# A pass for the maximum of a hidden layer: work of VectorE and ScalarE divided anew over three engines

## The reference, cut to what matters

```python
def bitnet_linear(x, W, b):
    w_scale = jnp.maximum(jnp.mean(jnp.abs(W)), 1e-05)
    qW = jnp.sign(W) * (jnp.abs(W) > 0.5 * w_scale).astype(W.dtype)
    i_scale = jnp.maximum(jnp.max(jnp.abs(x)), 1e-08) / 127.0
    qx = jnp.clip(jnp.round(x / i_scale), -128.0, 127.0)
    out = jnp.einsum('...i,oi->...o', qx, qW) * (w_scale * i_scale)
    return out + b
...
avg_img = jnp.mean(image_embeds, axis=1, keepdims=True)
concatenated = jnp.concatenate([fused, jnp.broadcast_to(avg_img, (b, s, e))], axis=-1)
h = jax.nn.relu(bitnet_linear(concatenated, W_f1, b_f1))     # 512 -> 1024
return bitnet_linear(h, W_f2, b_f2)                          # needs max |h| first
```

## Time and profile before

| | us |
|---|---|
| median of 3 runs | 1606.0 (1601.48 to 1606.73) |
| span of the profiled execution | 1604.8 |
| PE busy in it | 1374.0 (86%) |
| DVE busy | 1164.6 (73%) |
| ACT busy | 942.2 (59%) |
| POOL busy | 341.6 (21%) |
| the pass, from its first memset to its last reduction | 1194.94 to 1274.41 |

### The profile page before, as it was taken

The page is one execution under the profiler, slowest core; times in us unless marked ns, Lnnn a source line. Parts: engine busy times, 40 slices in busy tenths (PEclk is TensorE's granted clock), DMA queues, the critical chain, the costliest instruction groups (busy, mean ns, idle before and its releaser), DMA issues. The chain is left out here.

```text
span 1604.8 us, 25713 instructions
## 1 busy us (share of the span) xinstructions
PE 1374.0 (86%) x8272; PEld 1087.8 (68%) x8315; DVE 1164.6 (73%) x3017; ACT 942.2 (59%) x1434; POOL 341.6 (21%) x311
## 2 busy tenths in 40 slices
PE   8566779999999999999999777548868779999996
PEld 2345667888888888888888666435632247777775
DVE  6535666767887777778787844429969868898895
ACT  3333354566566675676656445369947057877873
POOL 2012111111221212121221100077200042433320
PEclk9767789999999999999999999869979889999998
DMA  7661033434554555445556675343200011111211
GB/s 218 144 234 39 25 118 124 141 129 151 180 165 146 173 163 164 151 148 165 173 174 223 204 227 169 131 128 108 60 2 0 5 48 40 61 60 54 67 53 40
DMA packets 114561, 192.64 MB, mean 120 GB/s; under 512 B 18256, under 2 KB 83360, under 8 KB 114400
## 3 DMA queue, kind: packets, MB, share of 16 engines
q1 hardware_dynamic: 96352, 146.18, 29.4%
q0 software_dynamic: 13824, 43.81, 7.9%
q10 hardware_dynamic: 4256, 1.07, 0.3%
HBM read 134.10 MB, written 57.98 MB: 120 GB/s over the span
## 5 line engine op out<-in xcount | busy, mean ns | idle before, releaser
L1268 ACT ACTIVATE hr_r<-pair 128x512 f32<-128x512 f32 x136 | 80.1, 592 | 141.4 <-PE pair L167 139.7
L165 PE MATMUL pair<-kv_ring,hr_lo 128*128 128x256 f32 x544 | 158.5, 291 | 4.1 <-DVE hr_lo L3216 4.1
L166 PE MATMUL pair<-kv_ring,hr_hi 128*128 128x256 f32 x544 | 154.3, 284 | 0.0
L167 PE MATMUL pair<-kv_ring,hr_hi 128*128 128x256 f32 x544 | 154.2, 284 | 0.0
L165 PE MATMUL pair<-th_hi,kv_ring 128*128 128x512 f32 x272 | 115.4, 424 | 42.1 <-issue 39.0
L4443 ACT ACTIVATE ff<-pair,hbs,s1h 128x512 f32<-128x512 f32 x128 | 96.4, 774 | 77.8 <-PE pair L4753 72.9
L4397 POOL DMA_INDIRECT ff<-x_scratch,slots x64 | 78.2, 1222 | 224.2 <-POOLq L3895 141.1
L1070 POOL DMA_INDIRECT rows_scratch<-row,slot x64 | 68.7, 1074 | 221.3 <-DVE slot L3155 163.5
L3216 DVE TENSOR_TENSOR hr_lo<-hr_sq,hr_hi 128x512 fp32r<-128x512 f32 x136 | 93.3, 688 | 26.9 <-ACT hr_sq L1282 12.6
L165 PEld LDWEIGHTS pair<-kv_ring,hr_lo 128*128 128x128 f32 x544 | 104.3, 192 | 10.6 <-DVE hr_lo L3216 5.4
L166 PE MATMUL pair<-th_lo,kv_ring 128*128 128x512 f32 x272 | 109.3, 402 | 0.0
(11 more groups left out here) (420 smaller groups left out, 4212.6 us busy)
## 6 DMA issues: line engine op xcount, KB each, us to landing
kv_ring<-expert_scratch SPq DMA_DIRECT2D x136, 512.0 KB, 3.9
acc_s<-rows_scratch SPq DMA_DIRECT2D x17, 528.0 KB, 5.3
xn_s<-rows_scratch SPq DMA_DIRECT2D x17, 512.0 KB, 5.0
x_scratch<-acc_s SPq DMA_DIRECT2D x17, 512.0 KB, 4.4
text_scratch<-text SPq DMA_DIRECT2D x17, 512.0 KB, 5.3
x_in<-in_x SPq DMA_DIRECT2D x16, 512.0 KB, 4.8
expert_scratch<-expert_space POOLq DMA_DIRECT2D x2, 4096.0 KB, 18.4
out<-ff SPq DMA_DIRECT2D x16, 512.0 KB, 2.9
```

The costliest lines, as they stand in the source:

```text
L165: pe.matmul(dst, st[1], mv[0], start=start, stop=False, skip_group_check=True)
L166: pe.matmul(dst, st[0], mv[1], start=False, stop=False, skip_group_check=True)
L167: return pe.matmul(dst, st[0], mv[0], start=False, stop=stop, skip_group_check=True)
L1268: s.activation(hr_r[:, c % 2, :], up_ps[:, (c % 2) * T:(c % 2 + 1) * T], ACT.Relu).then_inc(relu_done, 1)
```

## The change

The 16 samples, the matmuls and what is computed stay. The work after the matmuls and the rounding are divided otherwise:

- Pairs 0 and 1 (four chunks, `NR` = 4) are reduced by VectorE from PSUM as before.
- Pairs 2 and 3 are copied by **ScalarE** to SBUF as 16-bit integers (`whole`, two buffers; all values are whole numbers and fit). VectorE then halves them three times with an elementwise maximum (1024 elements a partition, 512, 256), each step waiting for the one before, and reduces the 256 that are left. This `fold` of sample n-1 stands behind the two reductions of sample n.
- The second rounding step, which subtracts the constant, goes to **GpSimd**. `qy` gets a second buffer. ScalarE's first step runs two samples ahead and stands in its list between the copies of two samples: rounded(n+2), then the copies of sample n.
- The copies of sample n wait until the fold of sample n-2 has freed their buffer. TensorE waits for pairs 2 and 3 on ScalarE's copies, for 0 and 1 on VectorE.
- All loops are written out.

```diff
-        qy = sb("qy", [P, KC * T])
+        qy = [sb(f"qy{h}", [P, KC * T]) for h in range(2)]
...
+                @block.gpsimd
+                def _(g):
+                    def quantised(n):
+                        g.wait_ge(hy_done, n + 1)
+                        g.tensor_scalar(qf[:, n, :, :].rearrange("p k t -> p (k t)"), qy[n % 2][:, :], ROUND, None, ALU.subtract).then_inc(hq_done, 1)
+                    for n in range(B):
+                        quantised(n)
...
-                        s.wait_ge(hy_done, n + 1)
-                        s.activation(qf[:, bass.ds(n, 1), :, :].rearrange("p o k t -> p (o k t)"), qy[:, :],
-                                     ACT.Identity, bias=neg_round[:, :]).then_inc(hq_done, 1)
...
+                    def evict(n):
+                        after(s, folded_, n - 1)
+                        for q in range(NR // 2, HC // 2):
+                            s.wait_ge(h_done, HC // 2 * n + q + 1)
+                            at = 2 * q - NR
+                            s.activation(whole_[n % 2][:, at:at + 2, :].rearrange("p c t -> p (c t)"), psum[q][:, :], ACT.Copy).then_inc(evicted, 1)
...
+                        if n + 2 < B:
+                            rounded(n + 2)
+                        evict(n)
...
+                    def fold(n):
+                        v.wait_ge(evicted, NE // 2 * (n + 1))
+                        w, st = whole_[n % 2], Steps(v, fold_steps, 3 * n)
+                        st.add(v.tensor_tensor(half_[:, :, :], w[:, :, 0:T // 2], w[:, :, T // 2:T], ALU.max))
+                        st.wait()
+                        st.link(v.tensor_tensor(quarter[:, :, :], half_[:, :, 0:T // 4], half_[:, :, T // 4:T // 2], ALU.max))
+                        st.link(v.tensor_tensor(eighth[:, :, :], quarter[:, :, 0:T // 8], quarter[:, :, T // 8:T // 4], ALU.max))
+                        v.tensor_reduce(hall[:, NR:HC, n:n + 1].rearrange("p c o -> p (c o)"), eighth[:, :, :], X, ALU.max).then_inc(folded_, 1)
```

More of the change, by code:

```diff
@@ L18 @@
 F32, F32R, BF16, I32 = mybir.dt.float32, mybir.dt.float32r, mybir.dt.bfloat16, mybir.dt.int32
+I16 = mybir.dt.int16
 ALU = mybir.AluOpType
@@ L4233, in build @@
             hy_done, hq_done, h_done, h_red = sem("hid_rounded"), sem("hid_quant"), sem("hid_f1"), sem("hid_reduced")
+            evicted, folded_, fold_steps = sem("hid_evicted"), sem("hid_folded"), sem("hid_fold_steps")
             neg_round, pos_round = sb("neg_round", [P, 1]), sb("pos_round", [P, 1])
+            NR = 4
+            NE = HC - NR
             hall = sb("hall", [P, HC, B])
+            whole_ = [sb(f"whole{h}", [P, NE, T], I16) for h in range(2)]
+            half_ = sb("half", [P, NE, T // 2], I16)
+            quarter = sb("quarter", [P, NE, T // 4], I16)
+            eighth = sb("eighth", [P, NE, T // 8], I16)
             qya = sb("qya", [P, KC, B])
@@ L4247, in _ @@
                     pe.wait_ge(acc_ready, 1)
[L4249 removed]
+                    for n in range(B):
+                        pe.wait_ge(hq_done, n + 1)
                         for q in range(HC // 2):
[L4251 to L4253 removed]
+                            if q < NR // 2:
+                                after(pe, h_red, NR // 2 * (n - 1) + q + 1)
+                            else:
+                                after(pe, evicted, NE // 2 * (n - 1) + q - NR // 2 + 1)
                             for c in (2 * q, 2 * q + 1):
@@ new lines, in _ @@
+                    s.wait_ge(round_set, 2)
+                    rounded(0)
+                    rounded(1)
+                    for n in range(B):
+                        if n == 2:
+                            s.wait_ge(l_loaded, 48)
+                            for k, name in enumerate(("rT", "kT", "vT")):
+                                s.activation(lw[name][0][:, :, :], lstg[:, k, :, :], ACT.Copy, scale=0.5 if name == "vT" else 1.0).then_inc(lhi_done, 1)
+                        if n + 2 < B:
+                            rounded(n + 2)
+                        evict(n)
@@ L4294, in _ @@
[L4294 to L4301, removed]
@@ new lines, in _ @@
+                    for n in range(B):
+                        if n == 2:
+                            for k, name in enumerate(("rT", "kT", "vT")):
+                                v.wait_ge(lhi_done, k + 1)
+                                v.scalar_tensor_tensor(out=lw[name][1][:, :, :], in0=lstg[:, k, :, :], scalar=0.5 if name == "vT" else 1.0,
+                                                       in1=lw[name][0][:, :, :].bitcast(F32), op0=ALU.mult, op1=ALU.subtract)
+                        for q in range(NR // 2):
+                            v.wait_ge(h_done, HC // 2 * n + q + 1)
+                            v.tensor_reduce(hall[:, 2 * q:2 * q + 2, n:n + 1].rearrange("p c o -> p (c o)"),
+                                            psum[q][:, :].rearrange("p (c t) -> p c t", c=2), X, ALU.max).then_inc(h_red, 1)
+                        after(v, folded_, n - 1)
+                        if n > 0:
+                            fold(n - 1)
@@ L4303, in _ @@
+                    fold(B - 1)
+                    v.wait_ge(h_red, NR // 2 * B)
+                    v.wait_ge(folded_, B)
                     v.wait_ge(acc_ready, 1)
```

22 lines of the change are left out of this document (5 added, 17 removed).

## The result

The changed kernel takes 1612.8 us (median of 20 runs, 1605.4 to 1623.9) where the kernel before takes 1605.2 (20 runs on the same chip, 1597.0 to 1611.5). The ratio is 1.0056 [1.0041, 1.0071], which is 9.0 us more, between 6.6 and 11.4 (the two medians lie 7.6 apart). It is slower.

A forecast was written before the change was run, and what follows sets the result against it. VectorE's reductions were taken as the bound. Steady saving -6.4, start costs +1.4, +0.3 and +0.1 gave -4.6; collisions +11.0 made +6.4 us, added to 1606.0 for 1612 us, range 1600 to 1618.

The forecast's parts named there:

- What bounds the pass: Steady part of the pass: VectorE's reductions are the bound, busy 65.30 of 65.30 us; TensorE waits for free pairs.
- The steady saving of 0.40 us a sample: VectorE: two PSUM reductions 2.26 plus fold 1.86 make 4.12 us against 4.52; sixteen samples save 6.4 us.
- The rival of 16-bit integers at the f32 rate: VectorE's halvings: 16-bit maxima run like f32, 0.93 us more a sample; 1616 without conflict, 1627 with; chance 0.07.
- The place of the collision: VectorE's fold: GpSimd asks for memory at 3.35 us, during the second halving, and the third waits, in samples 5 to 15.
- The margin: GpSimd's request at 3.35 us misses the gap by only 0.10; that much later, the third halving goes first.
- The size of a collision: Third halving waits for GpSimd's 1.2 us step to read its 1024 elements: 1.0 us a sample, 11 samples, +11.0 us.
- the old rule: VectorE and GpSimd sharing SBUF: the instruction that comes second is blocked for the whole of the first.
- The term for GpSimd's first step: Start of the pass: GpSimd's first step against ScalarE's 1.15 us, paid once, between -0.1 and +0.5, taken as 0.1.
- The idle time before the third reduction: Start of the pass: second reduction ends at 1202.45, third can start near 1203.8, so VectorE idles 1.4 us.
- The 0.3 us for the weight remainders: Start of the pass: three remainders wait for ScalarE's weight copies behind sample 1's copies; 0.3 us, between 0 and 0.7.
- The rival without a conflict: VectorE's fold: by phase the third halving goes first, or the exclusion does not bind VectorE; 1601.4 us, chance 0.33.
- A step of GpSimd of over 2 us would break the sum at that term.: Sign for the profile after: GpSimd's steps, expected near 1.2 us, would break the sum if over 2 us.

The follow-up runs named there:

- the one-input reduction: Against the changed kernel, the third halving left out and the second's 512 elements reduced directly: pass 73.84 us, ratio to the kernel before 0.9979.
- The later step: Against the changed kernel, GpSimd's step waits until the fold that ends a sample is through: pass 76.05 us, ratio to the kernel before 0.9990.

## Why the prediction was right, step by step

- **What bounds the pass.** Right. VectorE is the full engine before and after; GpSimd, ScalarE and TensorE cost time only where they delay VectorE.
- **The steady saving of 0.40 us a sample (4.12 for 4.52).** Right: 4.10 where nothing collides. Halvings of 0.683, 0.425 and 0.291 us against 0.693, 0.426 and 0.293 from the bf16 rows. The rival of 16-bit integers at the f32 rate fell with the first halving.
- **The place of the collision.** Right to the instruction. GpSimd's step begins 3.26 us into the sample (3.25 predicted), during the second halving, goes ahead of the third, which was due at 3.44 (3.45 predicted), and holds it, in 11 samples. The margin was put at 0.10 us, and 0.33 of the chances went to its other side, so that it held was no certainty. The phase did not drift, since ScalarE starts its copies from the end of the fold (it waited 19.3 us for it, in 11 times). Moving the step and nothing else gave 7.8 us back, and taking it away left all third halvings at 0.29.
- **The size of a collision.** Too large: 1.0 us predicted, 0.72 measured, so 8.0 us in place of 11.0. Two errors stood in it and worked against each other. GpSimd's step was put at 1.2 us, with bounds of 1.03 and 1.55, and takes 2.77, outside both: the price was taken from a step that writes and hardly reads, and from small ones, and the element count was carried over at a rate that does not hold for f32 read, subtracted and written as bf16. And the hold was put at the whole of the instruction, when it ends 0.90 us into it. The 1.2 us taken for the one stand near the 0.90 of the other by luck. With the true duration and the old rule the same sum would have been 11 x (2.77 - 0.15 - 0.05) = 28 us.
- **On the skill's rule.** The Trainium skill, SBUF — State Buffer, section Who interferes with whom, has the pair of instructions right: those with two SBUF inputs were held, and those from PSUM and the one-input reduction were not; and GpSimd was held in its turn (3.30 us for 2.77). That the block lasts for the whole of the other's instruction, the runs contradict: a halving started at 1230.76 under a step that ran to 1231.51, and took 0.68. The measurement decides. The skill's other figure, the 769 ns of the GPSIMD Engine Reference, section 3.1, from which 1.54 us was an estimate, is called a best case there; these runs have 1.49 us for 512 elements and 2.77 for 1024.
- **The start.** The term for GpSimd's first step was 0.1 us, at most 0.5; it was 1.75, as follows from the same mis-sized duration. The idle time before the third reduction was put at 1.4 and was 2.34: the two-pair start was computed as if TensorE came to full clock right behind its second pair, as in the kernel before. It came to it 5.5 us behind its first weight load, against 4.0 before. That is no sure effect of the change, since two kernels with the same start had 3.2 and 5.8 us, and idled 1.36 and 2.52 us there. The 0.3 us for the weight remainders was not needed.
- **The sum.** Predicted: -4.6 and +11.0, so +6.4. Measured in the pass: -4.2 + 1.75 = -2.5 without the collisions, +8.0 with them, so +5.5. The forecast of 1612 came near the measured 1612.8 for its mechanism, and partly because two errors of size offset each other: the collisions were overrated by 3.0 us, the start underrated by 1.65 + 0.94. The base helped too: the sum was added to 1606.0, the median of 3 runs, and that of 20 is 1605.2. The program's own difference, 9.0 us (6.6 to 11.4), is above the +6.4. The rival without a conflict was 4.6 us under before. The later step and the one-input reduction, which take the collisions away, measured 2.3 and 4.5 us under it in the pass, and 1.6 and 3.4 by the ratio.
- **"A step of GpSimd of over 2 us would break the sum at that term."** It did (2.77 us), and the sum survived because the hold ends 0.90 us into the step.

## What to carry to other kernels

Before work goes to GpSimd beside a chain of VectorE instructions with two SBUF inputs, draw one period of the loop with the start of each instruction, and look at what GpSimd's start falls upon: here the same step, moved by 1.1 us, cost 8 us or nothing. A start under a reduction from PSUM or from SBUF is free if the next instruction with two SBUF inputs is far enough behind: 0.9 us for a step of 1024 elements, while one that came 0.61 us behind was held for the other 0.29. Only reductions were tried as instructions with one SBUF input. An elementwise step of that kind is not shown to be free: in the kernel before, one of 0.17 us took 0.43 beside a step of GpSimd. The first item of a pipeline pays the latency of the slower engine once in full, so it may stay on the faster one, while the rest goes to the engine with time to spare.

## What the runs showed of the hardware

- GpSimd subtracts a constant from 1024 f32 elements a partition and writes bf16 in 2.77 us, and 512 in 1.49: 2.5 ns an element and 0.2 us beside. ScalarE takes 1.15 us for 1024.
- Such a step keeps a VectorE instruction with two SBUF inputs off for 0.90 us from its start with 1024 elements, and 0.47 with 512, and no longer; a reduction of SBUF (0.687 us, unmoved) and one of PSUM (1.217) are not kept off. In turn a step that started 0.27 us into a halving took 3.30 us in place of 2.77. GpSimd's step gets in between two VectorE instructions of which the second depends on the first (the third halving took 1.01 us for 0.29, and a second one 1.27 for 0.56).
- Elementwise maxima of 16-bit integers run at the rate of bf16 (0.683, 0.425 and 0.291 us for 1024, 512 and 256 elements); a copy of 1024 f32 elements from PSUM to 16-bit integers takes 1.02 us on ScalarE, like a copy to f32.
- With ScalarE at 39.20 of 40.00 us and VectorE folding three pairs, ScalarE's copies took 1.14 us at the median and up to 1.24. What stretches them was not tested.
- The granted clock stood at 0.50 (1.2 GHz) for 3.2 to 5.8 us behind the first weight load of the pass, and these two ends come from kernels with the same start and the same work up to there. No cause for the difference was tested. It moves the pass by about 1 us (1.36 against 2.52 us of idle time).
